# A transformer stack on one core: weight preparation moved into the first projection, and an earlier start of the first attention

## The reference, cut to what matters

```python
x = x + attn_a(layernorm(x), W_qkv, b_qkv, W_o, b_o)     # dense causal, 16 heads of 16
x = x + ffn(layernorm(x), w_gate, w_up, w_down)
x = x + attn_b(layernorm(x), W_qkv, W_out, b_out)        # local + strided causal, rope
x = x + ffn(layernorm(x), w_gate, w_up, w_down)          # the same three weights

def fp4_quant_dequant(x):              # blocks of 16 along the last dim
    scale = maximum(max(abs(xb)) / 6.0, 1e-12)
    return GRID[searchsorted(MID, abs(xb / scale))] * sign(xb) * scale
def fp4_linear(x, w): return fp4_quant_dequant(x) @ fp4_quant_dequant(w).T
def ffn(x, ...): return fp4_linear(silu(fp4_linear(x, w_gate)) * fp4_linear(x, w_up), w_down)
```

## Time and profile before

| | us |
|---|---|
| median of 3 runs | 3343.1 (3340.86 to 3345.84) |
| profiled execution, its own time | 3338.47 |
| its span, first to last instruction | 3336.7 |
| weight stage | 0 to 47.4 |
| first projection (pA) | 47.4 to 251.9 |
| dense attention, first matmul | 266.8 |
| PE busy | 3098.7 (93% of the span) |
| DVE busy | 2606.8 (78%) |

### The profile page before, as it was taken

One profiled execution on the slowest core, in us unless ns is written; L12 is line 12 of the kernel. 1 busy time (PEld: TensorE's weight loads), 2 busy tenths in 40 slices (PEclk: granted clock), 3 DMA queues, 4 the chain that ended last, 5 costly groups with the idle time before them and its releaser, 6 DMA issues. The chain is left out here.

```text
span 3336.7 us, 92235 instructions
## 1 busy us (share of the span) xinstructions
PE 3098.7 (93%) x34732; PEld 2145.9 (64%) x34828; DVE 2606.8 (78%) x5407; ACT 1746.1 (52%) x3395; POOL 1092.9 (33%) x1631
## 2 busy tenths in 40 slices
PE   3997999999999799999979969999999969999999
PEld 2654777777776477777755535565555537777776
DVE  6547999999997699999959955655655649999997
ACT  3653887788788333333326635555555533333333
POOL 2542121121122222222216654454454432222222
PEclk8996999999999899999989979999999979999999
DMA  3764434434432222222226664445445322222221
GB/s 112 229 218 99 106 90 103 103 90 107 99 89 66 84 85 86 85 86 85 82 70 205 198 161 112 103 110 115 102 108 112 82 72 81 85 85 86 87 87 51
DMA packets 390672, 351.79 MB, mean 105 GB/s; under 512 B 111814, under 2 KB 331846, under 8 KB 390214
## 3 DMA queue, kind: packets, MB, share of 16 engines
q1 hardware_dynamic: 390342, 347.10, 38.6%
HBM read 210.12 MB, written 135.27 MB: 104 GB/s over the span
## 5 line engine op out<-in xcount | busy, mean ns | idle before, releaser
L852 DVE TENSOR_REDUCE aA_nmax<-bank 128x1 f32<-128x512 f32 (+3 forms) x1216 | 714.6, 653 | 69.9 <-PE bank L911 63.6
L895 ACT ACTIVATE aA_prob<-bank 128x512 f32<-128x512 f32 (+1 forms) x1216 | 616.8, 581 | 208.1 <-PE bank L911 202.9
L911 PE MATMUL bank<-aA_ks,aA_qs 96*32 96x512 bf16 (+13 forms) x6144 | 513.0, 321 | 27.0 <-POOL aA_vq L829 24.2
L1279 DVE TENSOR_REDUCE aB_nmax<-bank 128x2 f32<-128x512 f32 (+1 forms) x512 | 324.0, 657 | 212.9 <-remote 120.4
L911 PE MATMUL bank<-aA_qs,aA_ks 99*32 99x512 bf16 (+11 forms) x6144 | 470.2, 314 | 3.5 <-ACT aA_prob L895 1.8
L836 POOL TENSOR_SCALAR_AFFINE_SELECT aA_prob<-aA_prob 128x512 f32<-128x512 f32 x256 | 160.9, 634 | 663.6 <-ACT aA_prob L895 663.6
L911 PE MATMUL bank<-aA_prob,aA_vq 128*32 128x512 f32 (+3 forms) x3072 | 355.9, 490 | 1.4 <-POOL aA_prob L836 0.9
L1342 ACT ACTIVATE aB_prob<-bank 128x512 f32<-128x512 f32 (+1 forms) x512 | 278.2, 572 | 107.9 <-PE bank L1373 103.5
L911 PEld LDWEIGHTS bank<-aA_ks,aA_qs 96*32 96x32 bf16 x6144 | 247.2, 96 | 131.7 <-DVE aA_nmax L852 44.6
L1373 PE MATMUL bank<-aB_ks,aB_qs 96*128 96x256 bf16 (+3 forms) x2048 | 244.7, 258 | 38.8 <-DMA aB_own<-own_d 28.6
L911 PEld LDWEIGHTS bank<-aA_qs,aA_ks 99*32 99x32 bf16 x6144 | 224.8, 96 | 57.1 <-ACT aA_prob L895 19.3
(11 more groups left out here) (240 smaller groups left out, 6497.4 us busy)
## 6 DMA issues: line engine op xcount, KB each, us to landing
parts_A<-pA_part SPq DMA_DIRECT2D x96, 256.0 KB, 3.3
aA_qs<-parts_A SPq DMA_DIRECT2D x192, 128.0 KB, 3.9
aA_ks<-parts_A SPq DMA_DIRECT2D x192, 128.0 KB, 4.0
parts_B<-pB_part SPq DMA_DIRECT2D x96, 256.0 KB, 2.6
aB_qs<-parts_B SPq DMA_DIRECT2D x192, 128.0 KB, 3.9
aB_ks<-parts_B SPq DMA_DIRECT2D x192, 128.0 KB, 4.0
o_A<-aA_o_sb SPq DMA_DIRECT2D x32, 512.0 KB, 3.0
o_B<-aB_o_sb SPq DMA_DIRECT2D x32, 512.0 KB, 3.1
```

The costliest lines, as they stand in the source:

```text
L852: nc.vector.tensor_reduce(dst, src, AX.X, ALU.max, negate=True).then_inc(s["m_taken"], 1)
L895: nc.scalar.activation(dst, src, ACT.Exp, scale=SCALE).then_inc(s["e_taken"], 1)
L911: return nc.tensor.matmul(out, lhsT, rhs, start=start, stop=True, skip_group_check=True)
L1279: nc.vector.tensor_reduce(dst, src, AX.X, ALU.max, negate=True).then_inc(s["max_taken"], 1)
```

## The change

The weight stage is gone. Its constants are split in two: four that the first projection needs (`first`: identity, A's qkv weights, two biases), loaded behind unit 0 of x, and the rest (`later`: the three weights and seven constants), loaded behind unit 1. DVE, ACT and PE wait for `first` before their first step of pA. The quantisation becomes `on_vector(t)` and `on_scalar(t)`, one piece at the end of each of DVE's and ACT's steps; the multiplication by the scale for g and u moves from POOL to DVE. The 44 transposes come behind PE's last step, four or two to a copy, in two banks; ACT copies 14 times. The bias rows come behind DVE's last step.

In both projections the store of v moves behind the six stores of the parts. In the dense attention PE's wait for POOL's ones moves to the first exponential unit, and the six loads of k for group 0 go from SP's list to ACT's.

```diff
+    def on_vector(self, dve, t):
+        if t in (1, 3, 7):       # g, u, d: tensor_reduce, tensor_scalar, reciprocal
+        ...
+        if t in (2, 4, 8):       # v2 = w * rinv (scalar_tensor_tensor)
+        ...
+        if t in (5, 9, 12):      # sum = max(mag, 1) + v2
+        ...
+        if t in (6, 10, 13):     # v2 = sum - max(mag, 1)
+        ...
+        if t in (11, 14, 15):    # w = v2 * s22 (tensor_tensor)
+        ...
+    def on_scalar(self, act, t):
+        if t in (3, 7, 11):      # mag = abs(v2)
+        ...
+    def turn(self, pe):
+        for i, (k, starts, cw, _) in enumerate(self.turns):
+            pe.wait_ge(self.quantised[k], 1)
+            if i >= 2:
+                pe.wait_ge(self.copied, i - 1)
+        ...
# project_stage, SP
                         sp.dma_start(xin[k.p][:, :, :], x_v[k.t]).then_inc(x_loaded[k.p], 16)
+                        if extra and k.t == 0:
+                            extra.load_first(sp)
+                        if extra and k.t == 1:
+                            extra.load_later(sp)
                     if (k := at(STORE)):
-                        sp.wait_ge(s["v_ready"], k.t + 1)
-                        sp.dma_start(v_v[k.t // 2, k.t % 2], vs[k.p][:, :, :, :]).then_inc(v_stored[k.p], 16)
                         for q in range(2):
                             for j in range(3):
                                 ...
+                        sp.wait_ge(s["v_ready"], k.t + 1)
+                        sp.dma_start(v_v[k.t // 2, k.t % 2], vs[k.p][:, :, :, :]).then_inc(v_stored[k.p], 16)
# attend_stage
-                for n in range(3):
+                for r in range(NP6):
+                    sp.dma_start(qs[0][r:KROWS:NP6, :, :], parts_v[Q_PART[r], 0, 0]).then_inc(qk_loaded[0], 16)
+                for n in range(1, 3):
                     load_qk(n)
# ACT
+                for r in range(NP6):
+                    act.dma_start(ks[0][r:KROWS:NP6, :, :], parts_v[K_PART[r], NG, 0]).then_inc(qk_loaded[0], 16)
# PE
+                    if n == 0 and i == 0:
+                        pe.wait_ge(s["ones_set"], RING + 2)
...
-                pe.wait_ge(s["ones_set"], RING + 2)
```

More of the change, by code:

```diff
@@ L160, in weight_stage @@
[L160 to L172, removed]
@@ new lines, in __init__, with load_first @@
+        self.turns = []
+        for k, out in (("g", wgT), ("u", wuT)):
+            for c in range(DC):
+                for i in (0, 4):
+                    self.turns.append((k, [j * D + c * P for j in range(i, i + 4)], P,
+                                       out[:, c, i * WROWS:(i + 4) * WROWS]))
+        for c, (c0, cw) in enumerate(F_CHUNKS):
+            self.turns.append(("d", [i * F + c0 for i in range(2)], cw, wdT[0:cw, c, :]))
+    def load_first(self, sp):
+        for dst, src in self.first_loads:
+            sp.dma_start(dst, src).then_inc(self.first, 16)
@@ new lines, in load_later, with wait_first, wait_later @@
+    def load_later(self, sp):
+        for k, src, parts in self.sources:
+            sp.dma_start(self.w[k][:, :].rearrange("p (a k) -> p a k", a=parts),
+                         src.rearrange("(a p) k -> p a k", p=self.rows[k])).then_inc(self.loaded[k], 16)
+        for dst, src in self.later_loads:
+            sp.dma_start(dst, src).then_inc(self.consts, 16)
+    def wait_first(self, eng):
+        eng.wait_ge(self.first, 16 * len(self.first_loads))
+    def wait_later(self, eng):
+        eng.wait_ge(self.consts, 16 * len(self.later_loads))
@@ new lines, in on_scalar @@
+    def on_scalar(self, act, t):
+        if t in (3, 7, 11):
+            i = (3, 7, 11).index(t)
+            k = "gud"[i]
+            act.wait_ge(self.steps[k], 4)
+            if i:
+                act.wait_ge(self.steps["gud"[i - 1]], 6)
+            self.nc.scalar.activation(self.mag[k], self.v2[k][:, :], ACT.Abs, scale=UP).then_inc(self.mag_made, 1)
+    def turn(self, pe):
[3 more added lines that the diff above has]
+                pe.wait_ge(self.copied, i - 1)
+            r = self.rows[k]
+            for j, c0 in enumerate(starts):
+                ins = self.nc.tensor.transpose(self.bank[0:cw, i % 2, j * r:(j + 1) * r], self.w[k][:, c0:c0 + cw],
+                                               self.ident[0:r, 0:r])
+            ins.then_inc(self.turned, 1)
@@ L275, in in_line, with copy_turned @@
+    def copy_turned(self, act):
+        for i, (k, starts, cw, dst) in enumerate(self.turns):
+            act.wait_ge(self.turned, i + 1)
+            self.nc.scalar.activation(dst, self.bank[0:cw, i % 2, 0:len(starts) * self.rows[k]],
+                                      ACT.Copy).then_inc(self.copied, 1)
 def in_line(count, last_lag, step):
@@ L290, in project_stage @@
         xin, xn = sb("xin", [P, A4, D]), sb("xn", [P, A4, D])
+        extra = Weights(nc, core, mem, bank, *weights) if weights else None
         st, mv = sb("st", [P, A4, 6]), sb("mv", [P, A4, 2])
```

212 lines of the change are left out of this document (102 added, 110 removed).

## The result

| | before | after | forecast |
|---|---|---|---|
| median, us | 3344.5 (4 runs, 3340.9 to 3349.2) | 3311.5 (4 runs, 3307.4 to 3315.8) | 3300.7 |
| ratio | | 0.9897, 95% interval 0.9881 to 0.9913 | |
| profiled execution, us | 3338.5 | 3309.8 | 3296.1 |
| its span, us | 3336.7 | 3308.1 | |

The change makes the kernel 1.0% faster. The median lies inside the forecast's range (3291 to 3313), 1.5 us from its upper end. The profiled execution of before lies at the fast end of its own spread, so from profile to profile the gain is 28.7 us, from median to median 33.0.

What follows compares the result with a forecast made beforehand. PE, busy 3098.7 of 3336.7 us, was taken as the bound, with two early holes to shorten. Terms -41.3 + 4.0 - 0.5 - 5.6 + 1.0 = -42.4 us gave a median of 3300.7, range 3291 to 3313.

Steps and rivals of the forecast that it cites:

- front, to the second block: Start of pA: with the weight stage gone, PE's second q and k block starts at 34.1 us, 41.3 earlier.
- granted clock behind the pause: PE gap of 2 to 3 us before the second q and k block; the sum had no term for a slower clock.
- pieces in pA: DVE's quantisation pieces in pA's steps leave PE waiting, 4.0 us in all; bounds 0 and 20.4.
- tail of pA: PE's last pA matmul to next stage: 8.8 us instead of 9.3, gain 0.5; bounds 4.5 gained, 1.5 lost.
- attention start: Dense attention: first matmul 9.4 us into its stage instead of 15.0, released by a DMA; 5.6 gained.
- pB: End of the second projection: the v store now comes behind the parts, 1.0 us lost (0 to 2.0).
- the landing of unit 2: Front of pA: unit 2 of x, queued behind the later loads, lands at about 25.1 us.
- a rival with a chance of 2%: Pauses from pieces keep pA's clock at the lower level, up to 11.2 us more a step; 3458; chance 0.02.
- followed through the chain, this leaves 0.45: pA: a 2.28 us two-tile piece makes add_bias 1.74 late, PE waits 0.45 us; seven such steps, 3.2 us.
- The rival that all lateness reaches TensorE: pA: each late add_bias reaches PE, 20.4 us instead of 4.0; 3317.1 us; chance 0.12.
- the floor of 4.3: End of pA: ACT's copies of 4352 columns for the weight turns take at least 4.3 us.
- The third rival's worry: Attention not earlier: 3306.3 us, chance 0.10; POOL's memsets slowing first reductions would at worst cost the same gain.

## Why the prediction came out as it did

Most mechanisms came as forecast, and their sizes did not: the total was 10.8 us too low from median to median, 13.8 from profile to profile. Two mechanisms were wrong. The clock behind the pause was put at nothing, and the second list for k was counted as a gain and costs time. All terms but one missed to the same side. That the median stayed inside the range is in part luck: the range's end is 12.3 us from the forecast. Term by term, in us:

| step | forecast | measured | |
|---|---|---|---|
| front, to the second block | -41.3 | -38.1 | mis-sized |
| granted clock behind the pause | 0 | +1.8 | left out |
| pieces in pA | +4.0 | +7.3 | mis-sized |
| tail of pA | -0.5 | -1.5 | inside its bounds |
| attention start | -5.6 | -2.7 | second list wrong |
| pB | +1.0 | +1.8 | inside its bounds |
| rest | 0 | +2.8 | within the spread of executions |
| sum | -42.4 | -28.6 | |

**The front.** The step that failed is the landing of unit 2, 25.1 us by the forecast, 28.78 by the trace. I let the later loads pass at the rate of the kernel before. From 8 to 20 us that kernel moved 293 GB/s and this one 212, at about the same share of the engines (1.01 and 1.04). SP issued unit 2 only at 19.14, behind 5.10 us for w_d and seven more loads, and I had taken no account of that either; but the engines hardly idled meanwhile, so the rate is what was short. Why the same loads went slower behind x no run shows. From the landing on, the forecast's 9.0 us to the block were 8.5. x and `first` came as said (8.74; 7.8 forecast).

**The clock.** The forecast gave it a place in a rival with a chance of 2%, but for gaps inside pA, not for the pause that it had itself put before the second block (2 to 3 us; it was 4.17). In nine kernels that pause is 3.79 to 6.30 us, and the step behind it is 1.8 us too long (3.79, 4.17, 4.31 and 4.76 us of pause) to 3.1 (5.06 us of pause, a step of 14.28 in the kernel with four banks). In the three kernels without the pause the clock stays at 1.00. The far side of that rival, every step at the lower level, did not come: with waits of some 0.5 us per step the granted clock stays at 1.00.

**The pieces.** The lateness of add_bias was nearly right: 1.74 us forecast, 2.15 measured (2.35 us behind the block instead of 0.20). What failed is "followed through the chain, this leaves 0.45": I followed one step that starts with TensorE as the bound. For such a step the order of size is right. In the kernel with less ahead of unit 2 a first two-tile piece left 0.16 (11.35), and in the changed kernel the first step, 61.95 - 50.29, is 0.47 over 11.19, behind the reduce of u with its small ones (0.8 forecast). But the next piece comes before the chain has recovered, the last cut, the piece, add_bias, the first cut and ScalarE's row close on themselves, and the period is the loop's length, 11.98 us: 0.79 a step. Eight of these, four of 0.12 and the first make the 7.3; the pieces over d, counted as nothing, are the four. The contention, which I had taken as the uncertain part, came nearly as counted: the piece ends at 64.38, the forecast's way gives 62.22 + 2.28 = 64.50. The rival that all lateness reaches TensorE (20.4) was wrong by more.

**The tail.** The turns took two banks' ping-pong, as forecast, at 0.57 us a group instead of 0.65. With four banks it is 2.0 us less, still above the floor of 4.3 that the forecast gave.

**The attention's start.** The step that failed is "with k on ACT's list the twelve are issued in half the time ... landing at +7.2 if the transfers keep up", with +9.4 taken. They do not keep up: 1.57 MB go at 157 to 212 GB/s, after a first microsecond in which nothing moves, whatever the lists. (The forecast's own terms, 7.7 and 2, also make 9.7 and not 9.4.) The forecast cited the Trainium skill (DMA: Bandwidth & Descriptors, "Issuing engines are not separate DMA queues") as speaking against the second list and priced it: the gain would stay at 3.9. Measured with one list: 15.0 - 11.0 = 4.0. The trace agrees with the rule, and I went against it because a DMA share of 0.85 seemed to leave room; with group 0 alone on two lists the mean share of the four full stretches is 0.86. With the second list the gain was less than 4.0, here 2.7: part of the difference is that SP was free early and set group 1's loads beside group 0's, the rest is open. The third rival's worry, POOL's memsets slowing the first reductions, was hardly tried: they start at 234.42 and the memsets end at 236.2; the first 42 took 24.00 us, the same as before.

**pB and the rest.** The v store costs 1.8, not 1.0, more than the whole 1.4 that the forecast gave its transfer. Of the last 2.8 us, 0.5 lie in the dense attention, 1.35 between its last matmul and pB's first, and 0.95 in the sparse attention. All thirteen kernels have the same instructions there and show 824.9 to 831.2, 643.1 to 645.4 and 744.5 to 749.1 us, so the 2.8 need no cause from the change, and none was shown.

## What to carry to other kernels

When work is put into an engine's list once per step, don't follow one late step: walk from an instruction to itself one step later, over the engines that are not the bound, and compare the loop's length with the step; the same 3.20 us cost 0.79 a step here in a row with ScalarE's work and nothing beside it. A pause of some 4 us on TensorE is to be priced with the slower clock behind it. Before loads are given to a second issuing engine, see whether the transfers or the issues set when the last one lands, and who issues into the gap that opens.

## What the runs showed of the hardware that I had not expected

- A VectorE pass with two SBUF inputs and POOL's addition take turns, at nearly full cost: the piece that starts at 61.18 lasts as if it began when POOL ends (62.22 + 2.16 = 64.38; undisturbed it takes 2.28), and POOL's next, at 62.50, as if it began when the piece ends (64.38 + 1.02 = 65.40; undisturbed 1.16). A one-input reduce of the same size beside the same addition cost neither anything (2.27 and 1.16).
- Loads keep the DMA engines about equally busy at very different rates: 386 GB/s at a share of 1.09 for x, some 210 at 0.95 to 1.10 while the weights pass (two of 88 rows, one of 128), 164 to 212 at 0.76 to 0.99 for q and k.
- The issue of one load took SP 0.43 us at one time and 5.10 at another (w_d, with 3.4 MB issued ahead of it, part of it landed).
- After a pause of 4.17 us the granted clock fell when TensorE was already busy again (block at 37.29, 0.70 from 38 to 39 us, 0.50 to 41). After one of 5.83 us, in the kernel with the pieces before the last cut, it had fallen before the block began at 37.49 (0.50 from 36 to 38).
